# Attention and mixture of experts on one Trainium2 core: other shapes and places for the weights' loads, the bias on GpSimd, the block list in parts

## The reference, cut to what matters

```
def _L0_xattn_ref(x, y, Wq, Wkv, Wproj, bproj):
    q = (x @ Wq).reshape(b, lq, H, DK).transpose(0, 2, 1, 3)
    kv = (y @ Wkv).reshape(b, lkv, 2, H, DK).transpose(2, 0, 3, 1, 4)
    k, v = (kv[0], kv[1])
    atten = jax.nn.softmax(jnp.einsum('bhid,bhjd->bhij', q, k) * SCALE, axis=-1)
    res = jnp.einsum('bhij,bhjd->bhid', atten, v)
    res = res.transpose(0, 2, 1, 3).reshape(b, lq, H * DK)
    return res @ Wproj + bproj
def _L0_ffn_ref(tokens, gate_w, expert_w, expert_b, combine_w):
    probs = jax.nn.softmax(jnp.einsum('bsh,eh->bse', tokens, gate_w), axis=-1)
    top2_w, top2_idx = jax.lax.top_k(probs, 2)
    expert_out = jax.nn.silu(jnp.einsum('nh,edh->ned', flat, expert_w) + expert_b[None, :, :])
    gathered = jnp.take_along_axis(expert_out, flat_idx[:, :, None], axis=1)
    mixed = jnp.sum(gathered * flat_w[:, :, None], axis=1)
    return jnp.einsum('bsh,dh->bsd', mixed.reshape(B, S, H), combine_w)
x = x + _L0_xattn_ref(_layernorm(x), ctx_768, Wq, Wkv, Wproj, bproj)
x = x + _L0_ffn_ref(_layernorm(x), gate_w, expert_w, expert_b, combine_w)
```

## Time and profile before

| | |
|---|---|
| median of three runs | 1642.24 us (1641.49 to 1644.45) |
| the profiled execution, time | 1642.6 us |
| its span, from the first to the last instruction | 1640.9 us |
| mean granted clock of TensorE | 0.975 |
| TensorE busy | 1514.8 us, 92% |
| VectorE busy | 1269.3 us, 77% |
| ScalarE busy | 1060.3 us, 65% |
| GpSimd busy | 877.2 us, 53% |
| DMA moved | 287.63 MB, 175 GB/s on average |

### The profile page before, as it was taken

One profiled execution on the slowest core, in us unless ns is written; L12 is line 12 of the kernel. 1 busy time (PEld: TensorE's weight loads), 2 busy tenths in 40 slices (PEclk: granted clock), 3 DMA queues, 4 the chain that ended last, 5 costly groups with the idle time before them and its releaser, 6 DMA issues.

```text
span 1640.9 us, 38420 instructions
## 1 busy us (share of the span) xinstructions
PE 1514.8 (92%) x11712; PEld 1453.6 (89%) x11712; DVE 1269.3 (77%) x3152; ACT 1060.3 (65%) x2890; POOL 877.2 (53%) x1182
## 2 busy tenths in 40 slices
PE   2399999999899999999999999999999999999796
PEld 2389999999899999999899999989999898999675
DVE  3388888888788888888877888877787788777666
ACT  3277777676566776777677667757776676766432
POOL 2165666656554555577665555556566455644410
PEclk8699999999999999999999999999999999999989
DMA  4363333333367777544577777557787777977822
GB/s 160 101 199 96 95 96 96 96 97 97 99 198 216 224 217 218 169 120 133 164 231 231 209 221 222 171 142 236 233 234 230 218 210 227 265 204 221 275 62 77
DMA packets 179805, 287.63 MB, mean 175 GB/s; under 512 B 23571, under 2 KB 114580, under 8 KB 179348
## 3 DMA queue, kind: packets, MB, share of 16 engines
q1 hardware_dynamic: 168852, 255.82, 53.9%
q0 software_dynamic: 10752, 29.37, 5.8%
HBM read 156.38 MB, written 61.60 MB: 133 GB/s over the span
## 4 chain that ended last, share of the span: by engine, by line
PE 73%; DVE 12%; issue 6%; ACT 4%; SPq 3%; POOL 1%; DMA 1%; ACTq 0%; DVEq 0%; POOLq 0%
PE gen_ps L564 20%; PE qk_ps L564 16%; PE o_ps L564 10%; PE proj_ps L564 10%; PE s_ps L564 8%; PE pT_ps L605 6%; PE gen_ps L688 1%; PE gen_ps L655 1%; DVE sums L1019 1%; PE gen_ps L663 1%; DVE neg_max L1012 1%; ACT stage L795 1%; DVE pT_s_lo L954 1%; SPq L500 1%; DVE xn L999 1%
## 5 line engine op out<-in xcount | busy, mean ns | idle before, releaser
L821 ACT ACTIVATE stage<-s_ps,neg_max 128x128 f32<-128x128 f32 x1024 | 292.8, 371 | 145.1 <-DVE neg_max L1012 120.6
L1331 POOL CAST o_s_hi<-stage 128x256 fp32r<-128x256 f32 x256 | 102.1, 399 | 479.2 <-ACT stage L795 475.3
L1322 POOL TENSOR_TENSOR stage<-stage,inv_sums 128x512 f32<-128x512 f32 x256 | 266.4, 1041 | 53.4 <-DVE inv_sums L1021 53.3
L564 PE MATMUL s_ps<-k_s,qk_s 128*128 128x256 f32 x1536 | 226.5, 283 | 39.1 <-DMA k_s<-qk_s 39.0
L564 PEld LDWEIGHTS s_ps<-k_s,qk_s 128*128 128x128 f32 x1536 | 201.6, 189 | 39.7 <-DMA k_s<-qk_s 39.7
L795 ACT CAST pT_s_hi<-pT_ps 128x512 fp32r<-128x512 f32 x256 | 150.8, 589 | 116.1 <-PE pT_ps L605 110.6
L1019 DVE TENSOR_REDUCE sums<-stage 128x4 f32<-128x512 f32 x256 | 172.8, 675 | 62.8 <-ACT stage L821 55.3
L1012 DVE TENSOR_REDUCE neg_max<-s_ps 128x4 f32<-128x512 f32 x256 | 174.0, 680 | 38.9 <-PE s_ps L564 38.9
L954 DVE TENSOR_TENSOR pT_s_lo<-pT_ps,pT_s_hi 128x512 fp32r<-128x512 f32 x256 | 171.8, 671 | 38.8 <-ACT pT_s_hi L795 35.7
L954 DVE TENSOR_TENSOR qk_s<-qk_ps,qk_s 128x512 fp32r<-128x512 f32 x256 | 175.6, 686 | 33.0 <-ACT qk_s L795 32.0
L1333 POOL TENSOR_TENSOR o_s_lo<-stage,o_s_hi 128x256 fp32r<-128x256 f32 x256 | 188.4, 736 | 21.0
(11 more groups left out here) (349 smaller groups left out, 4636.7 us busy)
## 6 DMA issues: line engine op xcount, KB each, us to landing
w_block<-expert_table SPq DMA_DIRECT2D x147, 512.0 KB
k_s<-qk_s SPq DMA_DIRECT2D x512, 128.0 KB
stage<-sorted_x SPq DMA_DIRECT2D x147, 128.0 KB
sorted_y<-stage SPq DMA_DIRECT2D x147, 128.0 KB
x_raw<-in_x SPq DMA_DIRECT2D x32, 256.0 KB
c_raw<-in_ctxT SPq DMA_DIRECT2D x32, 256.0 KB
stage<-in_x SPq DMA_DIRECT2D x32, 256.0 KB
x_kept<-x SPq DMA_DIRECT2D x32, 256.0 KB
```

Source lines behind the costliest of these rows:

```text
L564: mm = pe.matmul(out_ap, l, r, start=start and n == 0, stop=stop and n == len(terms) - 1, skip_group_check=skip)
L821: last = act.activation(probs[p % 2][:, k, :], s_ps[:, k * P:(k + 1) * P], ACT.Exp, bias=neg_max[p % 2][:, k:k + 1])
L1322: pool.tensor_tensor(probs[b][:, :, :], probs[b][:, :, :], inv_sums[b][:, :].unsqueeze(2).broadcast_to([P, 4, P]), ALU.mult).then_inc(prob ...
L1331: pool.tensor_copy(hi[:, :, :], o_full).then_inc(o_hi, 1)
```

## The change

Weights: wq's and wkv's key columns load in two pieces, those of the first two head pairs (FIRST, 256 columns) ahead of the values, the others (REST) behind them. The later pieces' low parts of wkv go from VectorE to GpSimd, and wproj is split by GpSimd alone (split_projection). TensorE waits for the REST pieces at head pair 2. The experts' loads leave the start for slots -1, 0 and 1, behind that slot's spread_keys; the second is 112 rows and 15 rows. The experts' splits and stores move by two slots, that of combine from slot 8 to slot 10.

Bias: pbias, its splits and the two matmuls go. bias_row holds the bias in all partitions, GpSimd's add_bias adds it to xb in slot 0 of the next pair, and add_residual waits for that (biased).

Block list: the clear_at copy stays in slot 7 (rows_end); count_blocks, list_blocks and list_outputs run in slots 0, 1 and 4 of the next pair.

```diff
+        FIRST, REST, VALUES = slice(0, 2 * P), slice(2 * P, D), slice(D, 2 * D)
         WEIGHTS = [
+            (in_wq[:, :, FIRST], raw_wq[:, :, FIRST]),
+            (wkv[0:P, FIRST], stage[:, 1, FIRST]),
+            (wkv_rest[:, FIRST], stage[:, 2, FIRST]),
+            (wkv[0:P, VALUES], stage[:, 1, VALUES]),
+            (wkv_rest[:, VALUES], stage[:, 2, VALUES]),
+            (in_wq[:, :, REST], raw_wq[:, :, REST]),
+            (wkv[0:P, REST], stage[:, 1, REST]),
+            (wkv_rest[:, REST], stage[:, 2, REST]),
             (wproj.rearrange("(g p) n -> p g n", p=P), stage[:, 3, :].rearrange("p (g n) -> p g n", g=HEAD_PAIRS)),
             (expertT[0:P, :], stage[:, 0, :]),
-            (expertT[P:2 * P - 1, :], stage[0:P - 1, 1, :]),
+            (expertT[P:2 * P - 16, :], stage[0:P - 16, 1, :]),
...
+        FOR_FIRST, FOR_VALUES, BY_VECTOR, PROJECTION, EXPERTS_FROM, COMBINE_SPLIT = 3, 5, 6, 8, 9, len(SPLIT) - 1
+        KEYS_BY_POOL = PROJECTION - BY_VECTOR
+        PROJ_BY_POOL = KEYS_BY_POOL + 1
...
             def load_weights(n):
-                if n in OVER:
-                    sp.wait_ge(w_lo_dve, OVER[n])
+                if n >= EXPERTS_FROM:
+                    sp.wait_ge(w_lo_dve, BY_VECTOR)
+                if n > EXPERTS_FROM:
+                    sp.wait_ge(w_lo_pool, KEYS_BY_POOL)
...
-            for n in range(5):
+            for n in range(EXPERTS_FROM):
                 load_weights(n)
...
+            sp.dma_start(bias_row[:, :], bproj.rearrange("(o c) -> o c", o=1).broadcast_to([P, C])).then_inc(bias_in, 16)
             load_ctx(1)
             load_x(1)
...
+                if s == -1:
+                    load_weights(EXPERTS_FROM)
+                if s == 0:
+                    load_weights(EXPERTS_FROM + 1)
+                    sp.dma_start(stage[P - 16:P - 1, 1, :], expertT[2 * P - 16:2 * P - 1, :]).then_inc(w_in[EXPERTS_FROM + 1], 16)
+                    sp.dma_start(stage[P - 1:P, 1, :], expert_b.rearrange("(o n) -> o n", o=1)).then_inc(
+                        w_in[EXPERTS_FROM + 1], 16)
+                    for e in range(RING):
+                        load_last(e)
+                if s == 1:
+                    load_weights(EXPERTS_FROM + 2)
+                if 2 <= s < E - RING + 2:
+                    load_last(s - 2 + RING)
+                if 2 <= s < E + 2:
+                    keep_expert(s - 2)
...
             (queries_keys, on TensorE)
+                if j == 0 and p == 2:
+                    pe.wait_ge(w_hi, PROJECTION)
+                    pe.wait_ge(w_lo_dve, BY_VECTOR)
+                    pe.wait_ge(w_lo_pool, KEYS_BY_POOL)
...
             (project)
-                    if p == HEAD_PAIRS - 1:
-                        terms.append((ones_s[:, :], pbias[:, :]))
...
             (add_residual, on VectorE)
-                dve.wait_ge(xres_in, (j + 1) * 16)
+                dve.wait_ge(biased, j + 1)
...
+            def rows_end(c, j):
                 dve.wait_ge(drained["rank"], j + 1)
+                dve.tensor_copy(clear_at[:, c, :], filled[:, 0:E]).then_inc(clear_ready, 1)
+
+            def count_blocks():
...
+            def list_blocks(c):
...
+            def list_outputs(c):
...
+                if i - 1 in plan.ends:
+                    if u == 0:
+                        count_blocks()
+                    if u == 1:
+                        list_blocks(plan.ends.index(i - 1))
+                    if u == 4:
+                        list_outputs(plan.ends.index(i - 1))
...
             (on GpSimd)
+            def add_bias(j):
+                pool.wait_ge(xres_in, (j + 1) * 16)
+                if j == 0:
+                    pool.wait_ge(bias_in, 16)
+                pool.tensor_tensor(xb, xb, bias_row[:, :].unsqueeze(1).broadcast_to([P, 2, C]), ALU.add).then_inc(biased, 1)
+
+            def split_projection():
+                pool.wait_ge(w_in[PROJECTION], 16)
+                raw, hi, _ = SPLIT[PROJECTION]
+                pool.tensor_copy(hi, raw).then_inc(wproj_hi, 1)
+                weight_lo(PROJECTION)
...
+                if u == 0 and before:
+                    add_bias(i - 1)
                 if i == -1 and u == 4:
-                    weight_lo(BY_VECTOR)
+                    for n in range(BY_VECTOR, PROJECTION):
+                        weight_lo(n)
+                    split_projection()
```

More of the change, by code:

```diff
@@ L178, in xattn_moe_kernel @@
         gate_last = sb("gate_last", [P, E])
-        pbias = sb("pbias", [P, C], F32R)
+        bias_row = sb("bias_row", [P, C])
         ident = sb("ident", [P, P])
@@ L209, in xattn_moe_kernel @@
         mT_s = hilo("mT_s", [P, 2, N2])
-        bias_raw = x1[0:1, 1, :]
-        bias_s = [y[0:1, :, :].rearrange("p a n -> p (a n)") for y in xbT[0]]
         last_row = sb("last_row", [P, RING, C])
@@ L296, in xattn_moe_kernel @@
         gen_ps = [stack.enter_context(nc.psum_tensor(f"gen_ps{b}", [P, 512], F32)) for b in range(BANKS)]
-        x_in, c_in, xres_in, gate_in, bias_in, ebias_in = (
-            sem(n) for n in ("x_in", "c_in", "xres_in", "gate_in", "bias_in", "ebias_in"))
-        w_in = [sem(f"w_in{n}") for n in range(9)]
+        x_in, c_in, xres_in, gate_in, bias_in, biased = (
+            sem(n) for n in ("x_in", "c_in", "xres_in", "gate_in", "bias_in", "biased"))
+        w_in = [sem(f"w_in{n}") for n in range(12)]
         table_stored = [sem(f"table_stored{r}") for r in range(RING)]
@@ L434, in keep_expert @@
                     sp.dma_start(expert_table[E * P:(E + 1) * P, :], of).then_inc(table_stored[e % RING], 16)
-            def keep_bias():
-                sp.wait_ge(ebias_lo, 1)
-                sp.wait_ge(zeroed, 2)
-                for h in range(2):
-                    sp.dma_start(pbias[h:h + 1, :].bitcast(F32), bias_s[h].bitcast(F32)).then_inc(bias_in, 16)
             def load_last(e):
@@ L639, in value @@
                 if n == 0:
[L640 to L641 removed]
+                    pe.wait_ge(w_hi, FOR_VALUES)
+                    pe.wait_ge(w_lo_dve, FOR_VALUES)
                 hi, lo = cT[j % 2]
@@ L806, in weight_hi @@
                 else:
-                    act.wait_ge(w_in[8], 16)
-                act.activation(hi, raw, ACT.Copy, scale=QSCALE if n == 0 else 1.0).then_inc(w_hi, 1)
+                    act.wait_ge(w_in[EXPERTS_FROM + 2], 16)
+                act.activation(hi, raw, ACT.Copy, scale=QSCALE if n in (0, FOR_VALUES) else 1.0).then_inc(w_hi, 1)
             def keys_values_ctx(j):
@@ L928, in _ @@
                 if i == -1 and u == 3:
-                    weight_hi(0)
+                    for n in range(FOR_FIRST):
+                        weight_hi(n)
                 general(s, "mid")
@@ L933, in _ @@
                 if i == -1 and u == 4:
-                    for n in range(1, BY_VECTOR):
+                    for n in range(FOR_FIRST, FOR_VALUES):
                         weight_hi(n)
                 if i == -1 and u == 5:
-                    act.wait_ge(ebias_in, 16)
-                    act.copy(bias_s[0], bias_raw).then_inc(ebias_hi, 1)
-                    weight_hi(BY_VECTOR)
-                if i == 0:
-                    weight_hi(EXPERTS_FROM + u)
+                    for n in range(FOR_VALUES, PROJECTION):
+                        weight_hi(n)
+                if 2 <= s < E + 2:
+                    weight_hi(EXPERTS_FROM + s - 2)
                 if i == 0 and u == 1:
@@ L944, in _ @@
                     act.copy(wgate[:, :, 0:E], gate_raw[:, :, :]).then_inc(gate_w_ready, 1)
-                if i == 1 and u == 0:
+                if i == 1 and u == 2:
                     weight_hi(COMBINE_SPLIT)
@@ L1210, in general @@
                         if n + 1 in plan.ends:
-                            list_blocks(plan.ends.index(n + 1), n)
+                            rows_end(plan.ends.index(n + 1), n)
             for e in range(REGIONS):
@@ L1255, in _ @@
                 if i == -1 and u == 3:
-                    weight_lo(0)
+                    for n in range(FOR_FIRST):
+                        weight_lo(n)
                 general(s, "mid")
@@ L1283, in _ @@
                 if i == -1 and u == 4:
-                    for n in range(1, BY_VECTOR):
+                    for n in range(FOR_FIRST, FOR_VALUES):
                         weight_lo(n)
+                if i == -1 and u == 5:
+                    weight_lo(FOR_VALUES)
                 if i == 0 and u == 0:
@@ L1301, in weight_lo @@
             def weight_lo(n):
-                pool.wait_ge(w_hi, n + 1)
                 raw, hi, lo = SPLIT[n]
+                if n == PROJECTION:
+                    pool.wait_ge(wproj_hi, 1)
+                else:
+                    pool.wait_ge(w_hi, n + (1 if n < PROJECTION else 0))
                 pool.tensor_tensor(lo, raw, hi.bitcast(F32), ALU.subtract).then_inc(w_lo_pool, 1)
@@ L1360, in _ @@
                 pool.memset(k_s[b][:, :, :, :].bitcast(F32), 0.0)
-            pool.memset(pbias[:, :].bitcast(F32), 0.0)
```

85 lines of the change are left out of this document (30 added, 55 removed).

## The result

The changed kernel takes 1590.65 us (median of four runs, 1589.83 to 1591.3) against 1642.93 us for the kernel before in the same job (1641.49 to 1644.45): a ratio of 0.9681 [0.9665, 0.9698]. The forecast was 1579.0 us. The profiled execution took 1589.83 us, its span 1588.0 us, with a mean granted clock of 0.990 (0.975 before). The span is 52.9 us shorter where I had summed 63. One run in all that follows stands apart: the profiled one of the kernel with the addition in slot 7 took 2445.29 us at a granted clock of 0.556, and the ratio leaves it out.

A forecast was written before the change was run, and what follows sets the result against it. TensorE bounds the kernel (73% of the chain), with its largest wait 38.6 us for k_s at the start. 39 + 7 + 17 = 63 us off the profiled 1642.6 gives 1579.6, against the median 1579; ends 1568 and 1597, range up to 1600.

The forecast's parts named there:

- The start: Part 1: spreading the 112 rows and loading first keys earlier ends the stall before the first scores; 39 us, between 33 and 44.
- The chain of GpSimd's four steps: At the start: two low parts, wproj's copy and its low part end last at about 29.3, when the first product starts.
- my 2.6: Start: total given back for experts' loads in slots -1 to 1, the 15 rows, late keys and similar; 2.6 us.
- one slot's keys come up to 2 us late, I take 0.6: Start: keep_expert's last stores (1 MB) now follow the clearing of the dump rows (0.9 MB), delaying one slot's keys; 0.6 us.
- The bias: Part 2: two matmuls fewer in slot 1 of 32 pairs, GpSimd's addition hidden; 7 us, between 2 and 8.
- Rival (c): Slots 0 and 1 of every pair: GpSimd's addition delays split and VectorE, 2.3 us a pair; time 1652, chance 0.03.
- The block list: Part 3: five calls' stalls, 22.6 us in all, less 5.6 given back in the next pair; 17 us, between 10 and 22.
- The 1.1 us that I gave back for each call: The list's steps still cost 1.1 us in the next pair, for each of 5 calls; 5.6 us back.
- the 3.5 us: Price of each of the three list calls that fall among other waits, between 0 and 6 us; 3.5 taken.
- the meeting with the addition: Slot 0 of five pairs: list and addition block each other once, up to 1.3 us each, 6.5 us, inside the bounds.
- (b): First two pairs: weights' pieces on GpSimd and loads in slots -1 to 9 cost some 13 us more; 1592, chance 0.12.
- (a): Start: the 112 rows stay on one engine at 25 GB/s, the start brings only 11.5 us; time 1606.5, chance 0.06.

## Why the prediction was right, and where it was wrong

**The start: 39 predicted, 33.75 measured.** That the load's shape was the stall holds (36.3 us alone, 35.0 lost when it is undone). The Trainium skill (DMA: Bandwidth & Descriptors, the section on why a DMA increments its semaphore by 16) has 112 rows in 16 parts and 127 in one; the trace agrees, with 129 to 315 GB/s against 23 to 34. For 15 rows no run here shows the number of parts: VectorE's first subtraction, which waits for all of the load, starts at 37.02 us after a wait of 0.3, and 4.9 us on one engine would have been over by then too. So of the 1.5 us that I kept for them no more than 0.3 shows there. The chain of GpSimd's four steps was nearly right: they began at 19.00 us (18.8 in my sum) and ended at 29.89 (29.3), as the first low part took 2.65 us, for a size that took 1.79 right after, and the copy of wproj 1.88, less than the 2.5 I took. But they did not end last: the first product, at 30.43, waited another 0.54 us for the inverse of the sums. From the first product to pair 0's residual addition it took 50.56 us for 48.25 before, inside my 2.6. **The step that failed** is the last: "one slot's keys come up to 2 us late, I take 0.6". Pair 1 was 4.3 us longer. I had seen that the stores now follow the clearing, and I had seen the addition on GpSimd, but had not put the second into the first: the addition stands ahead of the expert's low part for which the store waits. Either half taken away brings 3 to 4 us of it back (40.72 us with the addition in slot 5, 40.13 with the clearing moved). And a wait of 2.49 us cost more than itself, as TensorE's granted clock over that pair was 0.96.

**The bias: 7 predicted, 8.5 in the trace of the kernel with it alone, 6.3 by the median.** Right, also in what hides it: TensorE waits for GpSimd's stage or o_s_lo 1.1 us at most. Rival (c) had no ground in plain pairs.

**The block list: 17 predicted, 10.5 measured in its five pairs.** Alone it brings 20.7 (20.9 in its five pairs). The 1.1 us that I gave back for each call was right: the two clean calls bring 4.87 and 5.10 us (pairs 8 and 22) where I had 5.0 and 4.9. Too small was the 3.5 us, 2.4 after that, for each of the other three, which bring 4.79, 3.41 and 2.77. **The step that failed** is the weighing after it: I put the meeting with the addition at 1.3 us for each of five at most, called it inside the bounds, and took nothing for it in the likeliest value. It cost 10.4 us, about 2.1 each, since the step that is held starts during the scatter ahead of the addition, or just before the addition, and is released when the addition ends, and a later step is held once more (0.59 us for 0.17) beside GpSimd's split. The rule of the Trainium skill (SBUF — State Buffer, "Who interferes with whom"), which I had set beside the sum with 10.5, is borne out for the two-input step: 171 ns with the addition elsewhere, 2.14 us beside it in pairs 8 and 22. As I had put it, for steps with two inputs, it does not cover pairs 16, 26 and 28, where a one-input step is held. That its number fits to the tenth is partly luck, as both terms under it were too small. What I had named as its sign in the trace came too: TensorE waits of over 1.5 us for pT_s_lo, up to 1.9, in pairs 8, 16 and 22.

**The rivals.** The result, 1590.65, lies within my range (up to 1600) but 11.65 us above the 1579; the start (33.75) and the list (10.5) both lie just above the bad ends that I had given them, 33 and 10. It lies nearest to (b), 1592, "the start is paid back", but by another way: some 4 of the 11 us are the keys behind stores that it names, at 2; most of the rest is VectorE held in slot 0, which it had in its list at 6.5 as the port. I gave it 0.12. I let two meetings of parts that were each roughly priced count as unlikely. (a) and (c) did not come.

## What to carry to other kernels

Price the parts of a change alone, and then walk each slot in which two of them land. Here the three parts run alone gave 63.3 us and their sum without the meeting 63.8, and the loss was in two meetings, both of one 1.3 us instruction placed where another part had just moved. In this kernel a short chain of small VectorE steps should not share a slot with a GpSimd addition of 128x512; moving the addition by three slots was worth 14.3 us, more than a fifth of what the whole change brings at its best. And count rows before anything else when a load is slow: 127 rows cost 36 us here, 112 and 15 nothing that the traces show.

## What had not been expected of the hardware

**A small VectorE instruction can be held for longer than the GpSimd instruction beside it lasts.** The step top_w, four columns, takes 0.17 us on average in the kernels with no addition in slot 0, and 0.93 in the changed kernel, where it is held in 14 of its 32 calls (1.47 to 2.14 us). Its group there (us in all, mean ns), then VectorE's timeline in a pair with expert blocks, and GpSimd's:

```profile
L1103 DVE SCALAR_TENSOR_TENSOR top_w<-gate_exp,gate_inv 128x4 f32<-128x4 f32 x32 | 29.9, 933 | 1.1
```

```profile
435.57 2.13 DVE L1103 SCALAR_TENSOR_TENSOR top_w<-gate_exp,gate_inv 128x4 f32<-128x4 f32 x1
437.62 0.67 DVE L1026 TENSOR_REDUCE sums<-stage 128x4 f32<-128x512 f32 x1
...
435.25 1.07 POOL L1380 DMA_INDIRECT sorted_x<-xn,row_of  x1 [0.17 <-issue]
436.36 1.31 POOL L1366 TENSOR_TENSOR stage<-stage,bias_row 128x512 f32<-128x512 f32 x1
```

It starts 0.3 us into the scatter and ends with the addition, 2.13 us later. The same scatter without an addition behind it holds nothing: in the kernel with the list alone rows_new runs inside it in pairs 8, 16 and 22, at 171 ns. The starts of GpSimd's instructions are rough in the profile, so whether the hold begins with the scatter or with the addition is not shown. This one step is 24.4 of the 28.7 us by which VectorE's busy time grew, and it cost nothing: pairs with expert blocks take 45.28 us and 45.27 with the addition elsewhere. Held time only costs where a chain hangs on it.

**Not every VectorE instruction is held.** The sum over 512 columns (0.69 us) and the subtraction of an SBUF tile from a PSUM bank (pT_s_lo, 0.66) keep their length beside the addition. Steps of a few columns with two SBUF inputs are held, and so are those with a single SBUF input (rounded, 1.67 us at the fourth end for 0.29, and 1.98 for 0.17 at the second):

```profile
744.65 1.98 DVE L1174 TENSOR_SCALAR rounded<-rounded 128x9 f32<-128x9 f32 x1
```

Which property decides was not tried.

**The load of 127 rows stops the queue that issues.** With it in flight, the load issued next took 16.09 us to issue in its new place as it took 16.64 in the old one.
